# Masked sixteen-head attention: the mask is added on VectorE and on GpSimd instead of by matmuls

## The chip, the cores and the metric

The kernel runs on one core of one Trainium2 chip, as one launch. The metric is the device time of the program in microseconds. Five engines work beside each other, each through its own instructions in order: TensorE (PE in the profile; its weight loads are PEld), VectorE (DVE), ScalarE (ACT), GpSimd (POOL) and SyncE (SP), which issues the DMAs here. They wait for each other by semaphores. PE writes only to PSUM, eight banks of 128 x 512 float32; POOL works in SBUF.

## The reference

The program is a stack of twelve layers on a stream of 8 sequences of 256 tokens with 128 features. The change touches one of them, the second attention layer, which has 16 heads of 8 features and a causal mask:

```python
def _L1_attn_ref(x, w_qkv, b_qkv, w_out, b_out):
    N_HEADS = 16
    D_HEAD = D_MODEL // N_HEADS
    ...
    scores = jnp.einsum('bhqd,bhkd->bhqk', q, k) * scale
    causal = jnp.tril(jnp.ones((T, T), dtype=bool))
    scores = jnp.where(causal, scores, jnp.finfo(scores.dtype).min)
    attn = jax.nn.softmax(scores, axis=-1)
    out = jnp.einsum('bhqk,bhkd->bhqd', attn, v)
```

Two later layers have an attention of the same shape without a mask, over two members, and share the code.

## The kernel before

A class `SmallHeads` (L922) holds the attention of both kinds. `L1Attend` (L1268) is the masked one: `causal` is true, and there are 8 units, one for each sequence. The unmasked ones have 16 units each. All engines walk through one list of steps (`steps`, L974): step s belongs to unit s // 16 and head s % 16, and each engine emits its share of a step in the same order. So the order of the work is written out by hand, and an engine that waits holds up all its later work.

In the masked stage the 256 queries of a head are two blocks of 128, and the upper right block of the scores is never computed. A head has therefore three blocks of 128 columns: queries 0 with keys 0, queries 1 with keys 0, and queries 1 with keys 1. The first and the third need a triangular mask. The work of one unit goes like this:

- **Scores** (L1052 to L1064), one head in each step. PE writes the three blocks to bank 0 or 1, in turn. First a matmul of a bf16 identity (L1060) puts the mask table `mask_q` (0 or -3e38, 384 columns) into PSUM; two matmuls of 128 and 256 columns then add the scores. Before it writes, PE waits until the head two steps back has had its maximum taken (`topped`).
- **Maxima** (L1150): one DVE instruction for each head takes the maximum of each of the three blocks, from PSUM. After the last head, L1154 joins the second and third. POOL then splits the maxima into three bf16 parts (L1180 to L1186), PE turns them at step 3 of the next unit (L1023), and two DMAs add them as rows to the stacked keys and queries.
- **Shifted scores** (L1065 to L1080): at every odd step, 25 steps behind, PE computes the transposed scores less the maximum for a pair of heads, in banks 2 and 3 or 4 and 5, again with two mask matmuls first (L1075, table `mask_k`). ACT takes the exponential of both heads in one instruction (L1134) into one of four buffers `pt`.
- **Weighted values** (L1081 to L1097): once for two pairs, a quad, three steps behind its second pair, PE multiplies the exponentials with the values, sixteen matmuls.
- In between lie, on PE, the projections of a later unit (step 0), transposes (steps 5 and 9), the values (step 7) and the output (step 11); on DVE, the division at step 5 (L1159, L1162) and the addition to the stream at step 11 (L1306).
- POOL also splits queries and keys of a later unit into bf16 parts at step 0 (L1194 to L1201), behind the maxima.

SP carries the DMAs through DRAM that stack these parts. Stages are separated by a barrier of all engines.

## Time and profile before

| What | Value |
|---|---|
| Time, median of 3 runs | 2663.89 us |
| Lowest and highest run | 2650.3 and 2668.25 us |
| Time of the profiled execution | 2663.19 us |
| Span of the profiled execution, first to last instruction | 2661.4 us |
| Mean granted TensorE clock over the span | 0.877 |
| Busy: PE, PEld | 2029.5, 1075.7 us |
| Busy: DVE, ACT, POOL | 1438.6, 1142.0, 542.3 us |
| Masked stage, first maximum to last addition to the stream | 1351.5 to 1522.7 us |

The busy times are sums over the whole span, in which stages with very different loads follow each other. The granted clock is a share of 2.4 GHz; 0.5 is 1.2 GHz. Matmuls are pipelined, so a row's duration overlaps the next one's, and the time that a matmul takes from the engine is read from one start to the next. The profiled execution's own time exceeds its span by 1.8 us.

### The profile page before, as it was taken

How to read it: one execution, taken by the hardware profiler on the slowest of the kernel's cores; microseconds unless marked ns; L12 is line 12 of the kernel's file. 1: busy time of each engine (PE TensorE's matmuls, PEld its weight loads, DVE VectorE, ACT ScalarE, POOL GpSimd, SP SyncE). 2: the span in 40 equal slices, each digit the busy share in tenths (PEclk: the TensorE clock that was granted, in tenths of full speed). 3: DMA queues.
4: the chain of work that ended last, by engine and by line, in shares of the span. 5: the costliest groups of instructions: out<-in, count | busy, mean ns of one | idle time of the engine just before them, and what ended most of it. 6: DMA issues, size and time to landing. Idle time of an engine off the chain costs nothing.

```text
span 2661.4 us, 39085 instructions
## 1 busy us (share of the span) xinstructions
PE 2029.5 (76%) x15216; PEld 1075.7 (40%) x15216; DVE 1438.6 (54%) x2439; ACT 1142.0 (43%) x2404; POOL 542.3 (20%) x679
## 2 busy tenths in 40 slices
PE   6786877787877777868779965558798866689885
PEld 3444334433344523444334433224344443334444
DVE  4553465433555345533745367754677554477745
ACT  3454244421344424443424442223476623256761
POOL 2331134200233113320022000001332120223202
PEclk9998999888899799989879986788799977689997
DMA  3000000000000000000043000000544120154402
GB/s 134 1 1 1 0 1 1 1 0 0 1 1 1 1 0 1 1 1 1 0 91 61 2 0 0 0 0 8 106 83 88 23 64 0 33 97 79 91 7 80
DMA packets 50159, 70.97 MB, mean 27 GB/s; under 512 B 4980, under 2 KB 37972, under 8 KB 49464
## 3 DMA queue, kind: packets, MB, share of 16 engines
q1 hardware_dynamic: 47416, 60.07, 10.5%
q0 software_dynamic: 2560, 8.39, 1.0%
q8 instruction: 123, 2.02, 0.3%
q14 instruction: 60, 0.49, 0.1%
HBM read 50.59 MB, written 16.88 MB: 25 GB/s over the span
## 4 chain that ended last, share of the span: by engine, by line
PE 60%; DVE 20%; ACT 8%; issue 6%; POOL 4%; DMA 2%; SPq 0%; POOLq 0%; DVEq 0%; ACTq 0%
PE ps L196 57%; DVE arena L1150 3%; DVE arena L569 2%; PE ps L432 2%; ACT arena L516 1%; POOL arena L671 1%; POOL arena L664 1%; DVE arena L280 1%; ACT arena L269 1%; PE ps L1033 1%; DVE arena L642 1%; ACT arena L525 1%; DVE arena L915 1%; DVE arena L917 1%; ACT arena L270 1%
## 5 line engine op out<-in xcount | busy, mean ns | idle before, releaser
L196 PE MATMUL ps<-arena 128*18 128x256 f32 (+10 forms) x10088 | 716.1, 312 | 196.4 <-DVE arena L1150 47.7
L196 PEld LDWEIGHTS ps<-arena 128*18 128x18 f32 (+6 forms) x10088 | 388.0, 127 | 507.8 <-issue 180.3
L1150 DVE TENSOR_REDUCE arena<-ps 128x2 f32<-128x512 f32 (+1 forms) x640 | 396.3, 659 | 234.6 <-PE ps L196 232.0
L196 PE MATMUL ps<-arena,w_L0f 128*128 128x512 f32 (+3 forms) x800 | 356.1, 584 | 93.0 <-DVE arena L580 28.3
L1134 ACT ACTIVATE arena<-ps 128x1024 f32<-128x1024 f32 (+1 forms) x320 | 312.9, 981 | 132.9 <-PE ps L196 131.3
L516 ACT ACTIVATE arena<-ps,arena 128x128 f32<-128x128 f32 x512 | 227.0, 459 | 113.3 <-DVE arena L613 113.2
L196 PEld LDWEIGHTS ps<-arena,w_L0f 128*128 128x128 f32 (+2 forms) x800 | 153.1, 207 | 255.6 <-issue 160.2
L196 PE MATMUL ps<-arena,const 128*4 128x128 f32 (+2 forms) x1096 | 210.7, 416 | 35.9 <-ACT arena L1473 19.5
L671 POOL TENSOR_TENSOR arena<-arena 128x512 f32<-128x512 f32 x128 | 133.0, 1039 | 317.8 <-DVE arena L585 317.8
L569 DVE TENSOR_TENSOR arena<-ps,arena 128x1024 f32<-128x1024 f32 x128 | 152.6, 1219 | 64.1 <-PE ps L196 35.3
L525 ACT ACTIVATE arena<-ps 128x512 f32<-128x512 f32 x128 | 76.0, 598 | 225.3 <-PE ps L196 225.3
L663 POOL TENSOR_TENSOR arena<-arena 128x512 f32<-128x512 f32 x64 | 81.0, 1266 | 417.8 <-DVE arena L569 417.8
L196 PEld LDWEIGHTS ps<-arena,const 128*4 128x4 f32 (+2 forms) x1096 | 96.8, 108 | 141.3 <-issue 54.2
L280 DVE RECIPROCAL arena<-arena 4x128 f32<-4x128 f32 x80 | 67.7, 899 | 150.7 <-ACT arena L273 150.7
L432 PE MATMUL ps<-const,arena 128*128 128x128 f32 x512 | 91.5, 308 | 70.1 <-POOL arena L671 67.1
L580 DVE COPY arena<-ps 128x512 f32<-128x512 f32 x128 | 88.0, 688 | 96.1 <-PE ps L432 96.1
L196 PE MATMUL ps<-masks_b,ident_b 128*128 128x256 bf16 (+1 forms) x512 | 118.7, 315 | 25.9 <-ACT arena L516 15.1
L611 DVE TENSOR_REDUCE arena<-ps 128x8 f32<-128x1024 f32 x64 | 77.6, 1212 | 105.8 <-PE ps L196 105.4
L432 PEld LDWEIGHTS ps<-const,arena 128*128 128x128 f32 x512 | 64.9, 155 | 127.5 <-POOL arena L671 100.6
L516 ACT ACTIVATION_READ_ACCUMULATOR arena<-ps,arena 128x1 f32 x512 | 105.7, 206 | 0.0
L196 PE MATMUL ps<-arena,tilerow 4*128 4x128 f32 x672 | 88.2, 288 | 13.4 <-DVE arena L280 7.1
L196 PE MATMUL ps<-w_L0f,arena 128*128 128x512 f32 x192 | 97.6, 619 | 0.4
(231 smaller groups left out, 2403.5 us busy)
## 6 DMA issues: line engine op xcount, KB each, us to landing
scratch<-arena SPq DMA_DIRECT2D x40, 384.0 KB, 2.8
arena<-scratch SPq DMA_DIRECT2D x80, 192.0 KB
arena<-scratch SPq DMA_DIRECT2D x80, 128.0 KB
arena<-scratch SPq DMA_DIRECT2D x80, 88.0 KB
w_L0f<-in_L0f SPq DMA_DIRECT2D x2, 1557.0 KB, 12.4
arena<-arena SPq DMA_DIRECT2D x80, 12.0 KB
const<-in_const SPq DMA_DIRECT2D x1, 1276.0 KB, 7.9
residual<-in_x SPq DMA_DIRECT2D x1, 1024.0 KB, 5.0
```

What stands on the lines that cost most here:

```text
L196: return self.nc.tensor.matmul(o, lhsT, rhs, start=start, stop=stop, skip_group_check=True)
L280: V.reciprocal(r4, r4).then_inc(self.inverted.sem, 1)
L432: o = k.nc.tensor.transpose(k.ps[:, 6, (2 * j + t) * P:(2 * j + t + 1) * P], self.prob[G % 2][:, 2 * p + j, t, :], k.K("ident"))
L516: o = S.activation(self.prob[G % 2][:, j, t, :], k.ps[:, j, t * P:(t + 1) * P], ACT.Exp, bias=self.negm[G % 2][:, at:at + 1], scale=rn[:, ...
L525: self.k.nc.scalar.activation(self.sq[i % 4], self.k.ps[:, 4 + i % 2, :], ACT.Square).then_inc(self.squared.sem, 1)
L569: self.k.nc.vector.tensor_tensor(self.prod[n % 3].rearrange("p t (b s) -> p t b s", b=PER), x, tab, ALU.mult).then_inc(self.rotated.sem, 1)
L580: self.k.nc.vector.tensor_copy(self.probT[q % 4].rearrange("p j t s -> p (j t s)"), self.k.ps[:, 6, :]).then_inc(self.turn_copied.sem, 1)
L611: ch.did(V.tensor_reduce(self.mx[G % 2], ps[:, 0:4, 0:SEQ].rearrange("p j (t s) -> p j t s", t=2), AXX, ALU.max))
L663: G.tensor_tensor(y[:, i, :], first[:, 0, :], second[:, 1, :], ALU.add).then_inc(self.placed.sem, 1)
L671: self.k.nc.gpsimd.tensor_tensor(pr, pr, rinv, ALU.mult).then_inc(self.scaled.sem, 1)
L1134: S.activation(self.pt[g % 4][:, :, 0:both], ps[:, bank:bank + 2, 0:both], ACT.Exp, scale=self.scale).then_inc(self.exped.sem, 1)
L1150: V.tensor_reduce(self.mx[k % 2][:, :, at:at + 1], ps[:, i % 2, 0:SEQ + self.n1].rearrange("p (t s) -> p t s", t=self.blocks), AXX, ALU.ma ...
```

## The change

In the masked stage no matmul writes a mask any more.

For the maxima, DVE runs two instructions for each head in place of one. Each adds a part of the table `mask_q` (bf16, in SBUF) to the scores in PSUM, writes the sum as bf16 to a small buffer `masked`, and writes the maximum of the sums, with -3e38 as the start value, to one column: the first over 128 columns, the second over 256. That is one maximum for each block of queries, so L1154 and its flag `mx_joined` go.

For the exponentials, ACT exponentiates the unmasked shifted scores. POOL then overwrites, in place, the entries of the first and third block in which the key comes after the query with zeros, by one `affine_select` for each pair of 128 partitions x 512 float32. The weighted values wait for this (`selected`), and stand two steps further behind. POOL's loop runs over steps instead of units, and its splits stand at step 0, in the same order as before. The unmasked stages get the same instructions as before.

```diff
--- before.py
+++ after.py
@@ -925,6 +925,7 @@
 
 
 
+
     PAIRS, QUADS, LAG = HEADS // 2, HEADS // 4, 25
     STACKS, ROWS = STACKS, KD * len(SLOTS)
 
@@ -940,9 +941,9 @@
         self.qk = [a.take(2 * SEQ).rearrange("p (x s) -> p x s", x=2) for _ in range(2)]
         self.rest = a.take(2 * SEQ).rearrange("p (x s) -> p x s", x=2)
         self.parts = a.take_bf16(2 * PARTS * SEQ).rearrange("p (a s) -> p a s", a=2 * PARTS)
-        self.blocks = 3 if causal else 2
+        self.masked = a.take_bf16(2 * 3 * P).rearrange("p (e s) -> p e s", e=2)
         self.va = [a.take(2 * HEADS * 3 * (KD + 1)).rearrange("p (n d) -> p n d", n=2 * HEADS) for _ in range(3)]
-        self.mx = [a.take(self.blocks * HEADS).rearrange("p (t h) -> p t h", t=self.blocks) for _ in range(2)]
+        self.mx = [a.take(2 * HEADS).rearrange("p (t h) -> p t h", t=2) for _ in range(2)]
         self.mx_rest = a.take(2 * HEADS).rearrange("p (x g) -> p x g", x=4)
         self.mx_parts = [a.take_bf16(2 * PARTS * HEADS).rearrange("p (x a g) -> p x a g", x=4, a=PARTS) for _ in range(2)]
         self.mx_rows = [a.take_bf16(SEQ, PARTS * HEADS) for _ in range(2)]
@@ -958,9 +959,8 @@
         self.projected, self.biased, self.low = (self.sig(n, U) for n in ("projected", "biased", "low"))
         self.valued, self.v_copied = self.sig("valued", U), self.sig("v_copied", U)
         self.scored, self.topped = self.sig("scored", H * U), self.sig("topped", H * U)
-        self.mx_joined = self.sig("mx_joined", U)
         self.mx_split, self.mx_turned, self.mx_copied = (self.sig(n, U) for n in ("mx_split", "mx_turned", "mx_copied"))
-        self.shifted, self.exped = (self.sig(n, self.PAIRS * U) for n in ("shifted", "exped"))
+        self.shifted, self.exped, self.selected = (self.sig(n, self.PAIRS * U) for n in ("shifted", "exped", "selected"))
         self.weighed = self.sig("weighed", self.QUADS * U)
         self.raw_copied, self.turned, self.scaled, self.turned_again, self.ctx_copied = (
             self.sig(n, U) for n in ("raw_copied", "turned", "scaled", "turned_again", "ctx_copied"))
@@ -983,8 +983,9 @@
 
     def quad_at(self, s):
 
-        w = (s - self.LAG - 5) // 4
-        return w if s % 4 == 2 and 0 <= w < self.QUADS * self.units else None
+        s -= self.LAG + (7 if self.causal else 5)
+        w = s // 4
+        return w if s % 4 == 0 and 0 <= w < self.QUADS * self.units else None
 
     def is_unit(self, u):
         return 0 <= u < self.units
@@ -1056,11 +1057,9 @@
                     stacked = self.stacked[k % self.STACKS]
                     eng.wait_ge(stacked.sem, stacked.at(16 * self.loads * (k // self.STACKS + 1)))
                 self.wait_ge(eng, self.topped, s - 1)
-                if self.causal:
-                    mm(ps[:, e, 0:3 * P], k_.ident_b[:], k_.mask_q, stop=False)
                 for t in range(2):
                     keys = SEQ if t else self.n1
-                    o = mm(ps[:, e, t * self.n1:t * self.n1 + keys], q[rows, i // 2, t * P:(t + 1) * P], kk[rows, i // 2, 0:keys], start=not self.causal)
+                    o = mm(ps[:, e, t * self.n1:t * self.n1 + keys], q[rows, i // 2, t * P:(t + 1) * P], kk[rows, i // 2, 0:keys])
                 o.then_inc(self.scored.sem, 1)
             g = self.pair_at(s)
             if g is not None:
@@ -1070,18 +1069,15 @@
                     stacked = self.mx_stacked[u % self.STACKS]
                     eng.wait_ge(stacked.sem, stacked.at(32 * (u // self.STACKS + 1)))
                 self.wait_ge(eng, self.exped, g - 1)
-                if self.causal:
-                    for e in range(2):
-                        mm(ps[:, bank + e, 0:3 * P], k_.ident_b[:], k_.mask_k, stop=False)
                 for t, (st, cnt, at) in enumerate(((0, SEQ, 0), (SEQ - self.n1, self.n1, SEQ))):
                     for e in range(2):
                         rows = slice(64 * e, 64 * e + self.ROWS + PARTS)
-                        o = mm(ps[:, bank + e, at:at + cnt], kk[rows, x, t * P:(t + 1) * P], q[rows, x, st:st + cnt], start=not self.causal)
+                        o = mm(ps[:, bank + e, at:at + cnt], kk[rows, x, t * P:(t + 1) * P], q[rows, x, st:st + cnt])
                 o.then_inc(self.shifted.sem, 1)
             w = self.quad_at(s)
             if w is not None:
                 u, x = w // self.QUADS, w % self.QUADS
-                self.wait_ge(eng, self.exped, 2 * w + 2)
+                self.wait_ge(eng, self.selected if self.causal else self.exped, 2 * w + 2)
                 if w == 0:
                     self.wait_ge(eng, self.opened, 1)
                 if x == 0:
@@ -1147,11 +1143,13 @@
                 if i == 0:
                     self.wait_ge(eng, self.mx_split, k - 1)
                 at = self.PAIRS * (i % 2) + i // 2
-                V.tensor_reduce(self.mx[k % 2][:, :, at:at + 1], ps[:, i % 2, 0:SEQ + self.n1].rearrange("p (t s) -> p t s", t=self.blocks), AXX, ALU.max).then_inc(self.topped.sem, 1)
-                if self.causal and i == HEADS - 1:
-                    self.wait_ge(eng, self.topped, s + 1)
-                    mx = self.mx[k % 2]
-                    V.tensor_tensor(mx[:, 1, :], mx[:, 1, :], mx[:, 2, :], ALU.max).then_inc(self.mx_joined.sem, 1)
+                mx = self.mx[k % 2][:, :, at:at + 1]
+                if self.causal:
+                    for t, (st, end) in enumerate(((0, P), (P, 3 * P))):
+                        o = V.tensor_tensor_reduce(self.masked[:, i % 2, st:end], ps[:, i % 2, st:end], self.k.mask_q[:, st:end], 1.0, MASKED, ALU.add, ALU.max, mx[:, t])
+                else:
+                    o = V.tensor_reduce(mx, ps[:, i % 2, :].rearrange("p (t s) -> p t s", t=2), AXX, ALU.max)
+                o.then_inc(self.topped.sem, 1)
             u = k - 3
             if i == 5 and self.is_unit(u):
                 self.wait_ge(eng, self.turned, u + 1)
@@ -1167,16 +1165,18 @@
 
     def heads_gpsimd(self, eng, ch):
         G, U = self.k.nc.gpsimd, self.units
-        for k in range(-2, U + 1):
+        for s, k, i in self.steps():
+            g = self.pair_at(s)
+            if self.causal and g is not None:
+                pt = self.pt[g % 4][:, :, 0:3 * P].rearrange("p h (b c) -> p h b c", b=3)[:, :, 0:3:2]
+                self.wait_ge(eng, self.exped, g + 1)
+                G.affine_select(pt, pt, [[0, 2], [0, 2], [1, P]], ALU.is_ge, 0.0, base=0, channel_multiplier=-1).then_inc(self.selected.sem, 1)
             u = k - 1
-            if self.is_unit(u):
+            if i == 0 and self.is_unit(u):
                 mx, parts = self.mx[u % 2], self.mx_parts[u % 2]
-                if self.causal:
-                    self.wait_ge(eng, self.mx_joined, u + 1)
-                else:
-                    self.wait_ge(eng, self.topped, HEADS * (u + 1))
+                self.wait_ge(eng, self.topped, HEADS * (u + 1))
                 self.wait_ge(eng, self.mx_turned, u - 1)
-                mx = mx[:, 0:2].rearrange("p t (e g) -> p (t e) g", e=2)
+                mx = mx.rearrange("p t (e g) -> p (t e) g", e=2)
                 ch.did(G.tensor_copy(parts[:, :, 0, :], mx))
                 ch.wait_ge()
                 ch.did(G.tensor_tensor(self.mx_rest, mx, parts[:, :, 0, :], ALU.subtract))
@@ -1185,7 +1185,7 @@
                 ch.wait_ge()
                 G.tensor_tensor(parts[:, :, 2, :], self.mx_rest, parts[:, :, 1, :], ALU.subtract).then_inc(self.mx_split.sem, 1)
             u = k + 2
-            if self.is_unit(u):
+            if i == 0 and self.is_unit(u):
                 qk = self.qk[u % 2]
                 self.wait_ge(eng, self.biased, u + 1)
                 if u:
```

## Rows read from the trace of the kernel before

**Rows 1.** Busy us by stretch: PE, PEld, DVE, ACT, POOL; then the granted clock
```profile
1340.00:1360.00 20.00, 9.46 (x35) 3.18 (x34) 4.99 (x9) 1.24 (x3) 7.04 (x8) 0.50 0.65 140
...
1400.00:1420.00 20.00, 20.00 (x179) 8.59 (x177) 9.93 (x20) 9.17 (x14) 4.43 (x8) 1.00 0.30 64
1500.00:1520.00 20.00, 17.75 (x208) 7.87 (x206) 3.00 (x9) 12.30 (x18) 0.91 (x4) 1.00 0.01 3
```

**Rows 2.** The chain of waits in the masked stage: start us, length us
```profile
1412.24 14.57 PE ps L196 x128
```

**Rows 3.** Timeline of PE: start us, length us; two heads and a pair
```profile
1436.66 0.34 PE L196 MATMUL ps<-masks_b,ident_b 128*128 128x384 bf16 x1
1436.93 0.34 PE L196 MATMUL ps<-arena 48*128 48x128 bf16 x2
...
1437.73 0.50 PE L196 MATMUL ps<-masks_b,ident_b 128*128 128x384 bf16 x2
1438.17 0.34 PE L196 MATMUL ps<-arena 51*128 51x256 bf16 x4
1438.44 0.34 PE L196 MATMUL ps<-masks_b,ident_b 128*128 128x384 bf16 x1
```

**Rows 4.** Timeline of POOL: first instruction of the split of maxima, four units
```profile
1366.38 0.21 POOL L1180 CAST arena<-arena 128x32 bf16<-128x32 f32 x1 [11.30 <-DVE arena L1154]
...
1420.94 0.21 POOL L1180 CAST arena<-arena 128x32 bf16<-128x32 f32 x1 [14.70 <-DVE arena L1154]
...
1441.22 0.21 POOL L1180 CAST arena<-arena 128x32 bf16<-128x32 f32 x1 [14.70 <-DVE arena L1154]
...
1500.18 0.21 POOL L1180 CAST arena<-arena 128x32 bf16<-128x32 f32 x1 [18.20 <-DVE arena L1154]
```

**Rows 5.** Timeline of DVE: the first maximum of the masked stage
```profile
1351.51 0.56 DVE L1150 TENSOR_REDUCE arena<-ps 128x3 f32<-128x384 f32 x1 [19.04 <-PE ps L196]
```

**Rows 6.** Groups by form, masked stage: busy us, mean ns, idle before
```profile
L1150 DVE TENSOR_REDUCE arena<-ps 128x3 f32<-128x384 f32 x128 | 71.1, 559 | 89.5 <-PE ps L196 89.4
...
L1197 POOL TENSOR_TENSOR arena<-arena 128x512 f32<-128x512 f32 x8 | 9.2, 1155 | 0.6
...
L1194 POOL CAST arena<-arena 128x512 bf16<-128x512 f32 x8 | 4.9, 609 | 26.3 <-ACT arena L1109 17.4 <-DMA scratch<-arena 8.9
...
L1306 DVE SCALAR_TENSOR_TENSOR residual<-ps,cols,residual 128x256 f32<-128x256 f32 x8 | 3.8, 478 | 9.1 <-PE ps L196 9.1
...
L1162 DVE TENSOR_TENSOR arena<-ps,arena 128x256 f32<-128x256 f32 x8 | 3.4, 424 | 0.3
...
L1159 DVE RECIPROCAL arena<-ps 128x32 f32<-128x32 f32 x8 | 2.8, 351 | 9.6 <-PE ps L1033 9.6
```

**Rows 7.** Groups by form, whole kernel: operations near the new ones
```profile
L516 ACT ACTIVATION_READ_ACCUMULATOR arena<-ps,arena 128x1 f32 x512 | 105.7, 206 | 0.0
...
L285 DVE TENSOR_TENSOR arena<-arena,ps 128x512 f32<-128x512 f32 x64 | 41.4, 662 | 3.3 <-PE ps L196 3.1
...
L762 DVE SCALAR_TENSOR_TENSOR arena<-ps,cols,arena 128x512 f32<-128x512 f32 x32 | 24.0, 750 | 41.2 <-ACT arena L749 41.2
...
L627 DVE TENSOR_TENSOR stream<-stream,ps 128x256 f32<-128x256 f32 x32 | 13.4, 418 | 67.4 <-PE ps L196 67.4
...
L842 DVE TENSOR_TENSOR_SCAN arena<-arena 128x512 f32<-128x512 f32 x4 | 4.9, 1223 | 5.6 <-POOL arena L854 5.6
```

**Rows 8.** Timeline of POOL: split of maxima in the unmasked stage, two units apart
```profile
1927.16 0.21 POOL L1180 CAST arena<-arena 128x32 bf16<-128x32 f32 x1 [9.09 <-DVE arena L1150]
...
1957.16 0.21 POOL L1180 CAST arena<-arena 128x32 bf16<-128x32 f32 x1 [9.10 <-DVE arena L1150]
```

**Rows 9.** Busy us by stretch, unmasked stage, columns as in the first group
```profile
1920.00:1940.00 20.00, 17.98 (x196) 8.80 (x192) 14.55 (x25) 14.87 (x20) 4.44 (x8) 1.00 0.50 96
```

**Rows 10.** Busy us by stretch, earlier stages, columns as in the first group
```profile
380.00:400.00 20.00, 13.07 (x134) 8.21 (x134) 13.45 (x22) 9.86 (x34) 5.27 (x5) 1.00 0.00 1
860.00:880.00 20.00, 13.33 (x180) 9.90 (x180) 8.31 (x17) 6.50 (x28) 4.16 (x4) 0.83 0.00 1
```

## The prediction

> **What bounds the kernel now.** I read the time by stretch first. Only the masked attention layer changes, about 171 us of a 2661.4 us span. In its steady part PE is busy for all of 20.00 us, at a granted clock of 1.00, while DVE works 9.93, ACT 9.17 and POOL 4.43 us [rows 1]. The chain of waits agrees: it stays on PE for 14.57 us and 128 matmuls without a break [rows 2]. DVE waits for PE: 128 maxima of 559 ns are 71.1 us of work and 89.5 us of idle time in front [rows 6]. So the masked stage is bound by PE, and the question is what binds it when the mask matmuls are gone, and how soon.
>
> Its clock of units is the start of POOL's split of the maxima, which follows the last maximum of a unit: a unit takes 1441.22 - 1420.94 = 20.3 us, and the seven units after the first take 1500.18 - 1366.38 = 133.8 us [rows 4]. The first takes 1366.38 - 1351.51 = 14.9 us [rows 5]; it has only scores and maxima, at half the clock [rows 1]. After that comes a tail to 1522.7 us, 22.5 us, with shifted scores and weighted values alone.
>
> **What PE sheds.** From start to start, a head's mask takes 1436.93 - 1436.66 = 0.27 us, and a pair's two take 1438.17 - 1437.73 = 0.44 us [rows 3]. A unit has 16 heads and 8 pairs: 16 x 0.27 + 8 x 0.44 = 7.8 us. All of it lies on the path now. PE keeps 20.3 - 7.8 = 12.5 us of work in a unit. Nothing is added to PE.
>
> **What DVE takes on.** In place of 0.559 us for a head come two instructions, over 128 and over 256 columns, each with PSUM and SBUF as inputs. Two kinds of rows are near. A TENSOR_TENSOR with such inputs takes 0.418 us for 256 columns and 0.662 for 512, so 0.95 ns for a column and about 0.30 us for 128; the two together 0.72 us. A SCALAR_TENSOR_TENSOR takes 0.478 us for 256 and 0.750 for 512, 1.06 ns for a column, about 0.34 us for 128; together 0.82 us [rows 6, 7]. The first is the lower bound, and for the body I take the middle, 0.77. Keeping a running maximum should not slow it: today's maximum reads 384 columns in 0.559 us.
>
> Each of the two also has to write its maximum out. No DVE row shows that. On ACT the same thing is a row of its own, 0.206 us for one column [rows 7]. The bounds are 0 (it is part of the body, as in today's maximum) and 0.21 us for each; I take 0.1, since DVE's fixed cost is the smaller one: its body of 128 columns is 0.30 us in all. That makes 0.77 + 2 x 0.1 = 0.97 us for a head, with ends at 0.72 and 0.82 + 0.42 = 1.24.
>
> The Trainium skill says in "VectorE: DVE Perf Modes", section "Two Vector instructions with no wait between them", that an operation that also writes its accumulator is two instructions, the main one and an accumulator read. It gives no time for the read, and no trace here shows one on DVE; it speaks for the upper half of the range, and by it with ACT's price a head would cost about 1.2 us and the change would gain nothing.
>
> **The new unit.** DVE's other work in it is 0.35 + 0.42 + 0.48 = 1.25 us (L1159, L1162, L1306 [rows 6]). So DVE needs 16 x 0.97 + 1.3 = 16.8 us, more than PE's 12.5. PE is one head ahead of DVE (two banks), so it has about 2 x 0.97 us for a score of 0.27 and whatever stands beside it, and most insertions fit. The stage becomes bound by DVE. The join L1154 goes; it is worth 0.2 us, behind the last maximum, and nothing waits long for it.
>
> **POOL and the new wait.** A select reads one input of 512 elements. The nearest rows are POOL's one-input CAST of that size, 0.609 us, and its TENSOR_TENSOR, 1.155 us [rows 6]; below 0.6 nothing speaks for it, above 1.2 only an unknown. I take 0.85. Eight of them and today's 4.4 us [rows 1] are 11.2 us in a unit of 16.8. The wait falls on PE, in front of a quad, and behind it on PE stand all later scores. A quad stands five steps after its second pair, about 5 us, of which pair, ACT's exponential (0.8 us) and select use 2.2. It is tight once in a unit: at step 0 POOL does both splits, about 5 us, before it gets to the selects of steps 1 and 3, whose quad stands at step 8. POOL is then done at about 2.5 + 1.1 + 3.8 + 2 x 0.85 = 9.1 us after the last score of the unit before, and step 8 comes at 9 x 1.05 = 9.4. So I cost the wait at nothing; its cover is DVE's slowness, and if DVE is fast it may cost up to 0.5 us a unit. The later split of the maxima is not late either: it waits for the select of step 15 first, at most 0.85 us, and PE wants it only at step 3. SP's queue and its DMAs are untouched.
>
> The Trainium skill, "GPSIMD Engine Reference", section "4.1 Engine selection", calls one-input operations on GpSimd roughly line-rate and two-input ones about twice as slow; CAST and TENSOR_TENSOR here stand at 0.61 and 1.16 us, which agrees, and by it a select would be near 0.6. The sum would not move, as DVE sets the pace.
>
> **The sum.** First unit: 16 x 0.97 = 15.5 for 14.9 us, +0.6. The second and third have no division and no addition yet, 15.5 each, and the second stalls on projections at half the clock, for which I add 1.5: 32.5. The other five take 16.8: 84.0. Together 116.5 for 133.8, -17.3. The tail has 12 pairs; their masks are 12 x 0.44 = 5.3 us, but its PE is busy only 17.75 of 20 us and ACT 12.30 [rows 1], and the last select adds 0.85. Between -5.3 and +1 I take -2. Sum: 0.6 - 17.3 - 2 = -18.7 us. From the profiled execution's own 2663.19 us that gives 2644.5; the median before, 2663.89, is 0.7 above it, so I say **2645 us**. The change of slope is the thing to know: 0.1 us on a head of DVE is 128 x 0.1 = 12.8 us.
>
> **Rivals.**
>
> Fast DVE. The read-out is nearly free, a head costs 0.72 to 0.90 us. Then DVE's 16 x 0.8 + 1.3 = 14.1 us meets a floor. The unmasked stage shows it: two units take 30.0 us [rows 8], so 15.0 each, with PE at 17.98 and DVE at 14.55 of 20 us [rows 9], that is 13.5 and 10.9 in a unit. The hand-over costs 1.5 us beyond the busier engine. Here PE's 12.5 + 1.5 = 14.0 is the floor. Six units in 14.1 to 14.5 instead of the 118.5 they take now, and 2 to 3 us in the rest: -34 us, **2629**. For it speaks that all today's maxima are free of a second row.
>
> Dear DVE, slower than before. From 0.97 + 18.7/128 = 1.12 us a head the gain is gone, and from 1.32 the kernel is slower by over 1%. If the new instruction runs at the rate of TENSOR_TENSOR_SCAN, 1.223 us for 512 columns [rows 7] against 0.69 for other forms, 384 columns cost 0.4 us more: 1.37 us a head, -18.7 + 128 x 0.40 = +32, **2696**. Against it speaks the 0.559 us of today's maximum. This also covers that the "one instruction" is executed as several.
>
> Slow select. From (16.8 - 4.4 - 1.2) / 8 = 1.4 us a select POOL sets the pace (1.2 for its waits), through the wait in front of the quads. At 2.0 us a unit takes 21 to 22, about +8 us; at 2.4 it is 25 and **2695**. Against it speak both POOL rows; for it, only that no select is in the trace.
>
> Cold PE. With PE busy for 12.5 of 16.8 us the granted clock could stay at 1.2 GHz, as in the first unit. PE would need 23 to 25 us a unit: **2700**. In earlier stages 13.07 busy of 20 us go with a clock of 1.00, and 13.33 with 0.83 [rows 10], so dips are possible, but PE's own slack of 4 us covers these.
>
> **Chances.** Forecast (0.90 to 1.12 us a head, 2639 to 2664): 0.48. Fast DVE: 0.27. Dear DVE: 0.15, of which 0.06 beyond 1%. Slow select 0.06, half of it beyond 1%. Cold PE 0.04. A change under 1% (26.6 us) can hardly be told from none here, the runs before spread over 18 us. Faster by over 1%: the fast DVE and the lower edge of the forecast, 0.32. Slower by over 1%: 0.06 + 0.03 + 0.04 = 0.13. Within: 0.55. The range goes from the fast rival, 2629, less 2 for scatter, to 1.24 us a head, 2679: 2627 to 2680.
>
> **What would show it.** The two new rows on DVE and their sum for a head (0.97), any row for the read-out; DVE busy at over 18 of 20 us in the steady part and PE near 15; a unit of 16.8 us by POOL's splits; selects near 0.85 us, and no wait of PE for POOL above some tenths; the tail 2 us shorter. The prediction is wrong if a head on DVE is off by 0.1 us or more, if PE waits for POOL in every unit, or if the clock falls in the steady part.

## The result and the profile after

| | Before | After |
|---|---|---|
| Median beside each other, 4 runs each | 2661.99 us | 2619.82 us |
| Ratio to before, 95% interval | | 0.9834 [0.9802, 0.9865] |
| Profiled execution, span | 2661.4 us | 2615.4 us |
| Mean granted clock | 0.877 | 0.874 |
| First maximum to last addition | 171.2 us | 129.8 us |

The change makes the kernel 1.7% faster. The ratios are the recorded ones with their intervals; the quotient of the two medians, 0.984 here, lies inside the interval each time. One execution of e1_dve_part took 6265.98 us where its other three took 2620 to 2639, and it is left out below. 2645 was forecast; the time lies 7 us below the lower end of the range, and on the side of the fast-DVE rival (2629).

I read the profile after in the order in which the argument went before. First the time by stretch (columns: window, its length, busy us of PE, PEld, DVE, ACT, POOL with instruction counts, granted clock, DMA share, GB/s):

```profile
1340.00:1360.00 20.00, 10.68 (x46) 4.17 (x46) 10.57 (x71) 1.24 (x3) 5.98 (x10) 0.50 0.68 131
1360.00:1380.00 20.00, 18.32 (x142) 9.08 (x140) 13.76 (x91) 9.76 (x15) 11.88 (x19) 0.53 0.46 98
...
1400.00:1420.00 20.00, 16.13 (x216) 9.02 (x204) 14.84 (x95) 11.90 (x20) 15.16 (x26) 1.00 0.41 81
1420.00:1440.00 20.00, 16.49 (x214) 8.67 (x208) 15.55 (x99) 12.57 (x19) 8.09 (x16) 0.91 0.25 53
```

In the steady part nobody is busy all the time: PE has fallen from 20.00 of 20 us [rows 1] to 16.1, and DVE stands at 14.8, not at the 18 that a DVE-bound stage would show. The clock comes later than before: read in stretches of 2 us, it reaches 1.00 about 18 us after the first maximum in the kernel before and about 34 us after it here. The chain of waits (start us, length us) says the same. One unbroken piece of PE [rows 2] has become an alternation:

```profile
1398.98 1.54 PE ps L196 x22
1400.52 0.02 issue
1400.55 1.21 DVE arena L1149 x8
1401.76 0.05 issue
1401.81 1.11 PE ps L196 x18
...
1405.33 1.90 PE ps L196 x26
```

The clock of units, the start of POOL's split of the maxima, against [rows 4]:

```profile
1357.41 0.21 POOL L1180 CAST arena<-arena 128x32 bf16<-128x32 f32 x1 [6.94 <-DVE arena L1149]
...
1399.64 0.21 POOL L1180 CAST arena<-arena 128x32 bf16<-128x32 f32 x1
...
1413.37 0.21 POOL L1180 CAST arena<-arena 128x32 bf16<-128x32 f32 x1
...
1454.75 0.21 POOL L1180 CAST arena<-arena 128x32 bf16<-128x32 f32 x1
```

A steady unit takes 1413.37 - 1399.64 = 13.7 us for 20.3; seven units take 97.3 for 133.8, which is -36.5. The first, from the first maximum at 1346.46, takes 10.95 for 14.9: -3.9. The tail takes 21.5 for 22.5: -1.0. Together -41.4. The span of the profiled execution is 46 us shorter. The other 4.6 are 5.0 gained ahead of the first maximum and 0.4 lost behind the stage, where but for a fraction of a microsecond nothing is changed: in the experiments below, except e14, all with the same code ahead of the stage, the first maximum comes anywhere from 1340.9 to 1351.0 us. The two medians lie 42.2 us apart, about what the stage gave.

Now the rows that answer to the costs, groups by form in the masked stage (busy us, mean ns):

```profile
L1149 DVE CUSTOM_DVE_ANT_0 arena<-ps,masks_b 128x256 bf16<-128x256 f32 x128 | 53.7, 419 | 0.0
...
L1173 POOL TENSOR_SCALAR_AFFINE_SELECT arena<-arena 128x512 f32<-128x512 f32 x64 | 40.4, 637 | 43.8 <-ACT arena L1130 43.5
L1149 DVE CUSTOM_DVE_ANT_0 arena<-ps,masks_b 128x128 bf16<-128x128 f32 x128 | 36.9, 288 | 43.9 <-PE ps L196 43.0
...
L1149 DVE DVE_READ_ACCUMULATOR2_ANT arena<- 128x1 f32 x256 | 21.2, 83 | 0.0
```

By durations a head costs 288 + 83 + 419 + 83 = 873 ns, within a tenth of the 0.97 us that I forecast. But the timeline of DVE (start us, length us) shows how these rows lie:

```profile
1397.15 0.42 DVE L1149 CUSTOM_DVE_ANT_0 arena<-ps,masks_b 128x256 bf16<-128x256 f32 x1
1397.49 0.09 DVE L1149 DVE_READ_ACCUMULATOR2_ANT arena<- 128x1 f32 x1
1397.49 0.29 DVE L1149 CUSTOM_DVE_ANT_0 arena<-ps,masks_b 128x128 bf16<-128x128 f32 x1
1397.70 0.08 DVE L1149 DVE_READ_ACCUMULATOR2_ANT arena<- 128x1 f32 x1
1397.70 0.42 DVE L1149 CUSTOM_DVE_ANT_0 arena<-ps,masks_b 128x256 bf16<-128x256 f32 x1
1398.05 0.08 DVE L1149 DVE_READ_ACCUMULATOR2_ANT arena<- 128x1 f32 x1
```

The next instruction begins before the row in front of it has ended, and the read-out begins at the same moment as the next instruction. From start to start the 128 columns take 0.21 us and the 256 columns 0.35: **0.555 us for a head**. That is what the single maximum took, 0.559 [rows 6]. DVE needs 16 x 0.555 + 1.25 = 10.1 us in a unit, less than PE's 12.5. PE itself is busy for 11.6 of the 13.7 us, so even 12.5 was high by this measure.

So neither engine sets the 13.7 us alone. The waits between 1380 and 1460 us (engine, line, waited for: us in total, times, longest) show what is left of PE's idle time:

```profile
POOL arena L1173 <- ACT arena L1130: 33.1, 36, 2.1
...
PE ps L196 <- DVE arena L1160: 6.9, 5, 1.4
...
PEld ps L196 <- POOL arena L1186: 5.5, 6, 1.9
...
PE ps L196 <- POOL arena L1186: 3.7, 3, 1.6
...
PEld ps L196 <- POOL arena L1173: 0.9, 6, 0.2
```

Once a unit PE stands 1.4 us at step 7, for the division of DVE. The split of the maxima, wanted at step 3, makes PE wait 1.0 to 1.6 us only at the start of the last two units and of the tail; in the steady units only weight loads wait for it, 0.37 us. PE does not wait for the selects (0.9 us for weight loads, in six pieces). POOL waits for ACT, so the selects are early enough.

### The profile page after: what moved, and what is told of

Same layout as the page of the kernel before. It is cut to its first block, busy times and chain, and to the rows that moved or that the text cites. A ratio compares the mean times of both kernels' runs of the same rounds, so it can differ in the third digit from the quotient of the medians.

```text
span 2615.4 us, 39014 instructions
## 1 busy us (share of the span) xinstructions
PE 1962.8 (75%) x14960; PEld 1058.9 (40%) x14960; DVE 1442.4 (55%) x2815; ACT 1140.4 (44%) x2404; POOL 582.3 (22%) x743
## 4 chain that ended last, share of the span: by engine, by line
PE 58%; DVE 21%; ACT 8%; issue 7%; POOL 4%; DMA 2%; SPq 0%; POOLq 0%; DVEq 0%; ACTq 0%
PE ps L196 54%; DVE arena L1151 3%; DVE arena L569 2%; PE ps L432 2%; ACT arena L516 2%; POOL arena L671 1%; POOL arena L664 1%; DVE arena L280 1%; ACT arena L269 1%; PE ps L1034 1%; DVE arena L642 1%; ACT arena L525 1%; DVE arena L915 1%; DVE arena L1149 1%; DVE arena L917 1%
## 5 line engine op out<-in xcount | busy, mean ns | idle before, releaser
L196 PE MATMUL ps<-arena 128*18 128x256 f32 (+10 forms) x10088 | 699.1, 314 | 216.8 <-DVE arena L1151 47.6
L1151 DVE TENSOR_REDUCE arena<-ps 128x2 f32<-128x512 f32 x512 | 325.6, 686 | 145.5 <-PE ps L196 143.0
L1149 DVE CUSTOM_DVE_ANT_0 arena<-ps,masks_b 128x128 bf16<-128x128 f32 (+1 forms) x256 | 76.3, 354 | 43.9 <-PE ps L196 43.0
```

The lines of the kernel that those rows point to most:

```text
L196: return self.nc.tensor.matmul(o, lhsT, rhs, start=start, stop=stop, skip_group_check=True)
L1149: o = V.tensor_tensor_reduce(self.masked[:, i % 2, st:end], ps[:, i % 2, st:end], self.k.mask_q[:, st:end], 1.0, MASKED, ALU.add, ALU.max, ...
L1151: o = V.tensor_reduce(mx, ps[:, i % 2, :].rearrange("p (t s) -> p t s", t=2), AXX, ALU.max)
```

## The experiments

Theory A: DVE's real price of a head is 0.555 us, start to start, so DVE does not bind, and PE's missing 7.8 us of mask matmuls become time up to the waits for POOL's split and the division. Rival B (my forecast): DVE costs 0.9 us and more and sets the pace; the gain then came from elsewhere, a warmer clock or a shorter unit for another reason. Rival C: the select or its later quad decides.

All figures beside the ratios are from the profiled execution of each, in us: the first unit from first maximum to split, the seven units after it (the second to the eighth in the text), the stage from first maximum to last addition.

| Kernel | Median | Ratio to before, 95% | First unit | Seven units | Stage |
|---|---|---|---|---|---|
| before | 2661.99 | 1 | 14.9 | 133.8 | 171.2 |
| after | 2619.82 | 0.9834 [0.9802, 0.9865] | 10.95 | 97.3 | 129.8 |
| e1_dve_part | 2631.86 | 0.9856 [0.9782, 0.993] | 10.96 | 108.6 | 142.5 |
| e2_pool_part | 2653.2 | 0.9954 [0.9925, 0.9983] | 14.87 | 123.5 | 159.8 |
| e3_one_by_one | 2653.46 | 0.9966 [0.9939, 0.9992] | 14.7 | 130.3 | 167.4 |
| e4_third_instruction | 2666.81 | 1.0006 [0.9976, 1.0037] | 15.02 | 135.7 | 173.0 |
| e5_select_twice | 2637.57 | 0.9919 [0.9891, 0.9947] | 10.94 | 115.5 | 151.5 |
| e6_quad_lag5 | 2644.38 | 0.9936 [0.9909, 0.9962] | 10.95 | 117.0 | 156.9 |
| e7_quad_halves | 2627.19 | 0.9874 [0.9812, 0.9937] | 10.95 | 103.8 | 137.3 |
| e8_no_select | 2615.53 | 0.9831 [0.9776, 0.9885] | 10.94 | 97.2 | 127.3 |
| e9_split_first | 2631.33 | 0.9819 [0.98, 0.9839] | 10.94 | 99.4 | 130.0 |
| e10_split_first_turn4 | 2623.52 | 0.9796 [0.978, 0.9813] | 10.95 | 95.5 | 126.4 |
| e11_third_and_filler | 2680.18 | 1.0019 [0.9996, 1.0042] | 17.05 | 135.6 | 174.2 |
| e12_third_small_filler | 2677.81 | 1.0058 [1.0029, 1.0088] | 15.02 | 151.7 | 188.0 |
| e13_changed_again | 2625.75 | 0.9857 [0.9814, 0.99] | 10.95 | 100.0 | 132.3 |
| e14_split_turn_warm | 2618.23 | 0.984 [0.9803, 0.9876] | 14.68 | 89.6 | 123.7 |
| e15_split_turn_again | 2611.14 | 0.982 [0.9785, 0.9856] | 10.95 | 96.8 | 127.2 |

The kernel before took 2657.7 to 2675.43 us beside these, by the chip; medians of different groups (e1 to e4, e5 to e8, e9 to e11, e12 to e15) are compared by their ratios only.

**The two halves of the change.** Changed kernel, mask matmuls of the pairs back, no select:

```diff
+                if self.causal:
+                    for e in range(2):
+                        mm(ps[:, bank + e, 0:3 * P], k_.ident_b[:], k_.mask_k, stop=False)
...
-            if self.causal and g is not None:
+            if False and g is not None:
```

> Only the maxima are changed: the new DVE instructions and no mask_q matmuls; the mask_k matmuls stay, POOL selects nothing, quads three steps behind as before. Theory (a head costs DVE 0.56 us from start to start, so PE stays the bound and each PE saving counts fully): PE sheds 16 x 0.27 = 4.3 us of a 20.3 us unit, units of 16.0 to 16.2 us, first unit about 4 us shorter as in the changed kernel, about -33 us against the kernel before, 2629. Rival (a head costs DVE 0.87 us, the sum of its four rows): units of 16 x 0.87 + 1.3 = 15.2 us would still hide under PE, first unit 14 us instead of 11, so about -30. The two lie close here; the run is for what the maxima alone are worth beside the whole change. A second rival: POOL's part is what gave the time, and this run stands within 10 us of the kernel before.

The other half: the old maximum with its mask matmul and join, but the select of POOL:

```diff
+                    mm(ps[:, e, 0:3 * P], k_.ident_b[:], k_.mask_q, stop=False)
...
+                V.tensor_reduce(self.mx[k % 2][:, :, at:at + 1], ps[:, i % 2, 0:SEQ + self.n1].rearrange("p (t s) -> p t s", t=self.blocks), AXX, ALU.max).then_inc(self.topped.sem, 1)
```

> Only the exponentials are changed: no mask_k matmuls, POOL selects, quads five steps behind; the maxima are as before, with mask_q matmuls and the join. Theory: PE sheds 8 x 0.44 = 3.5 us of a 20.3 us unit, but the hand-over between PE and DVE shows again as PE has less to do; units of 16.8 to 17.7 us, first unit unchanged at 14.9, about -18 to -23 us against the kernel before, 2640 to 2645. Rival (POOL's select and its wait cost PE time): units stay above 18.5 us and the gain under 12 us.

Time by stretch, first of e1, then of e2:

```profile
1400.00:1420.00 20.00, 19.97 (x210) 9.37 (x204) 13.59 (x86) 11.52 (x18) 5.28 (x12) 1.00 0.44 81
```

```profile
1400.00:1420.00 20.00, 19.24 (x195) 9.69 (x194) 11.52 (x24) 10.99 (x18) 11.60 (x24) 1.00 0.31 65
```

With DVE's two instructions alone the unit is 15.75 us and PE is full; DVE at 0.97 us a head would have made it 16.8. Here DVE has 5 us of slack in a unit. With the select alone the unit is 16.82, which is 20.3 less eight pairs of 0.44. Both are in the main bound by PE (it is idle for 0.8 of the 16.82 us), and both sizes of what PE sheds were about right: 20.3 - 4.3 = 16.0 forecast for e1, 15.75 measured. The stage saves 28.7 and 11.4 us, together 40.1 of the change's 41.4, but this sum is partly luck. In a steady unit the halves save 4.5 + 3.5 = 8.0 us and the whole change only 6.6, as its waits come in; and e2 loses 6.6 us in its second and third units, which grow from 15.26 and 19.01 us to 19.03 and 21.80. There PE is busy all the time at a clock of 0.50 and 0.66, where the kernel before had 0.90 and 1.00. Without them e2's stage would be 18 us shorter, the lower end of what was expected. Why the clock came later there is open. The first unit's 3.9 us come with the DVE part alone.

**DVE at the price that I forecast.** In e3 each of DVE's instructions waits for the one before:

```diff
                 if self.causal:
+                    self.wait_ge(eng, self.topped, s)
                     for t, (st, end) in enumerate(((0, P), (P, 3 * P))):
                         o = V.tensor_tensor_reduce(...)
+                        if t == 0:
+                            ch.did(o)
+                            ch.wait_ge()
```

> The changed kernel with a wait in front of each of the two DVE maxima, so that each starts only when the one before it, its read-out included, has completed. Theory (what the forecast missed is that the rows overlap: a head is 0.288 + 0.083 + 0.419 + 0.083 = 0.87 us by durations but 0.555 us from start to start): with the overlap forbidden a head costs 0.87 us plus two semaphore delays of about 0.05, 0.97 us, which is the forecast's own figure; units of 16 x 0.97 + 1.3 = 16.8 us, first unit 15.5, about +25 us against the changed kernel, 2645. Rival (the forecast failed elsewhere, for instance because DVE is not what bounds the stage at such a cost): under +10 us.

```profile
1416.03 0.29 DVE L1150 CUSTOM_DVE_ANT_0 arena<-ps,masks_b 128x128 bf16<-128x128 f32 x1
1416.25 0.08 DVE L1150 DVE_READ_ACCUMULATOR2_ANT arena<- 128x1 f32 x1
1416.36 0.42 DVE L1150 CUSTOM_DVE_ANT_0 arena<-ps,masks_b 128x256 bf16<-128x256 f32 x1
1416.71 0.08 DVE L1150 DVE_READ_ACCUMULATOR2_ANT arena<- 128x1 f32 x1
1416.94 0.29 DVE L1150 CUSTOM_DVE_ANT_0 arena<-ps,masks_b 128x128 bf16<-128x128 f32 x1
```

The rows are as long as in the changed kernel, 0.29, 0.08, 0.42 and 0.08, yet the head now takes 1416.94 - 1416.03 = 0.91 us instead of 0.555. So the durations say nothing of the pitch; the overlap does. Two units of this kernel, by stretch:

```profile
1413.10:1429.30 16.20, 12.33 (x144) 6.84 (x136) 12.63 (x67) 8.52 (x14) 9.26 (x17) 0.92 0.39 79
1429.30:1450.20 20.90, 17.31 (x162) 8.33 (x160) 12.70 (x68) 8.95 (x14) 9.45 (x18) 0.65 0.30 61
```

The first is what I forecast, 16.2 us for 16.8, with PE's 12.3 of 12.5 in it. In the second DVE works the same 12.7 us, but the granted clock is at 0.65, PE's work stretches from 12.3 to 17.3 us, and the unit takes 4.7 more. The clock fell with PE idle for 3.9 of 16.2 us. My "cold PE" rival, given 0.04, is a real mechanism once DVE sets the pace. It is not confined to that case: the changed kernel's seventh unit stands at 0.88, and at 0.79 in e13.

**A third instruction**, the 256 columns once more, into a buffer that nobody reads, without a wait:

```diff
+                        if t:
+                            V.tensor_tensor_reduce(self.again[:, i % 2, :], ps[:, i % 2, st:end], self.k.mask_q[:, st:end], 1.0, MASKED, ALU.add, ALU.max, self.mx_again[:, i % 2:i % 2 + 1])
```

> The changed kernel with a third DVE maximum for each head, over 256 columns, into a buffer that nothing reads, between the two. Theory (price from start to start, 0.345 us for the 256-column one): a head costs 0.90 us, DVE 16 x 0.90 + 1.3 = 15.7 us of a unit and becomes the bound, units of 15.7 to 16.3, about +16 to +19 us against the changed kernel, 2636 to 2639. Rival (price by durations, 0.50 us more on 0.87): 1.37 us a head, units of 23 us, over +60 us.

```profile
1412.57 0.42 DVE L1151 CUSTOM_DVE_ANT_0 arena<-ps,masks_b 128x256 bf16<-128x256 f32 x1
1412.91 0.08 DVE L1151 DVE_READ_ACCUMULATOR2_ANT arena<- 128x1 f32 x1
1412.91 0.42 DVE L1152 CUSTOM_DVE_ANT_0 arena<-ps,masks_b 128x256 bf16<-128x256 f32 x1
```

```profile
1420.00:1440.00 20.00, 16.10 (x146) 8.14 (x146) 15.45 (x98) 8.90 (x14) 8.94 (x16) 0.67 0.32 64
```

The third costs its 0.35 us, as theory A says. What was expected of the time (2636 to 2639) failed: the clock is at 0.67 in the steady part and all of the change's gain is gone, though DVE is busy for only 15.5 of 20 us.

**Can the clock be held by filler?** e11 adds to e4 a matmul of 384 columns ahead of each head's scores, e12 one of 128 columns from the second unit on:

```diff
+                if self.causal:
+                    mm(ps[:, e, 0:3 * P], k_.ident_b[:], k_.mask_q)
...
+                if self.causal and k:
+                    mm(ps[:, e, 0:P], k_.ident_b[:], k_.mask_q[:, 0:P])
```

> The kernel with a third DVE instruction for each head (units of 19 to 20.5 us at a granted clock of 0.67, 2667 us), with one more matmul of 384 columns on PE in front of each head's scores, whose result the scores overwrite. It is work added: 16 x 0.27 = 4.3 us a unit for PE at full clock. Theory (in that kernel the excess over DVE's 15.7 us a unit comes from PE at 1.2 GHz, which falls there because PE is idle too often): PE stays at 2.4 GHz, its 12.5 + 4.3 = 16.8 us is the bound, units of 16.8 to 17.5 us, and the kernel gets faster by 10 us or more through added work, to 2645 to 2655. Rival (the excess is DVE's instruction or the hand-over, not the clock): slower than without the filler, 2667 or more.

> The kernel with a third DVE instruction for each head (units of 19 to 20.5 us, granted clock 0.67), with a small filler on PE: a matmul of 128 columns in front of each head's scores from the second unit on, about 0.12 us at full clock, 1.9 us a unit; the scores overwrite its result. The filler of 384 columns brought the clock back to 1.00 for part of the stage and units from 20.5 to 18.3 us, but cost PE 4.3 us a unit itself. Theory (the excess over DVE's 15.7 us is PE at 1.2 GHz, and a little more work on PE holds it at 2.4 GHz): units of 15.8 to 16.8 us wherever the clock reads 1.00, 15 us or more off the kernel without filler, about 2645 to 2650. Rival: the clock stays at 0.67, units of 20 us or more, 2667 or more.

```profile
1420.00:1440.00 20.00, 18.08 (x135) 9.11 (x136) 15.04 (x92) 8.10 (x12) 6.70 (x11) 0.65 0.33 64
```

No: in e12 PE is busy for 18.1 us and the clock stays at 0.65. From the fourth on, the units grow from e4's 19.2 to 20.5 to 22.6 to 23.7 us, though DVE has no more to do. So at that clock PE is in the main the bound (busy for 21.3 of 23.3 us), which is why slack on PE is no cover. With 384 columns the clock is at 1.00 in the middle (units of 18.3 us), but the filler costs as much as it brings, and e11 ends where e4 did.

**The select and its quad.** e5 runs the select twice, e8 never, e6 sets the quad back to its old distance, e7 computes it in two halves, two steps apart:

```diff
+                ch.did(G.affine_select(pt, pt, [[0, 2], [0, 2], [1, P]], ALU.is_ge, 0.0, base=0, channel_multiplier=-1))
+                ch.wait_ge()
...
-        s -= self.LAG + (7 if self.causal else 5)
+        s -= self.LAG + 5
...
-                    for f in range(4):
+                    for f in (range(2 * half, 2 * half + 2) if self.causal else range(4)):
```

> The changed kernel with every select run twice, the second behind the first. Each takes 0.64 us, so a pair costs POOL about 1.3 us and a unit 8 x 1.3 + 4.9 = 15.6 us. Theory A (POOL has slack now, with 8 x 0.64 + 4.9 = 10.0 of 13.7 us, but none for twice the work): POOL's wait in front of the quads becomes the bound, units of 15 to 16 us, about +12 to +15 us against the changed kernel, 2632 to 2635. Theory B (the quads' wait is far from the path, as the forecast costed it at nothing): under +3 us.

> The changed kernel with quads three steps behind their second pair, as before the change, instead of five. Theory: the exponential (0.8 us) and the select (0.64 us) do not fit in three steps of 0.86 us, and after POOL's splits at step 0 the selects are late, so PE waits for POOL in every quad or at least once in a unit; units of 15 to 16.3 us, +9 to +15 us against the changed kernel. Rival: PE's queue has slack of 2.5 us in a unit that takes this up, under +3 us.

> The changed kernel with the sixteen matmuls of a quad in two halves of eight, one for each pair, five steps behind the pair and two steps apart. Theory (the unit of 13.7 us is PE's 12.5 us of work plus a hand-over between PE and DVE, which shows because a whole quad, 0.78 us, stands between two scores while only two banks hold scores; half of it, 0.4 us, would fit beside a maximum of 0.555 us): units of about 13.2, -4 us against the changed kernel. Rival (earlier first halves run into POOL's splits, and the wait takes the place of the hand-over): units of 14 us or more, +3 us or more.

> The changed kernel without the selects: the quads wait for the exponentials alone, five steps behind, and the exponentials of masked places enter the weighted sums. This leaves POOL's new work and wait out. Theory (they are off the path while each select takes 0.64 us, but the split of the maxima stands behind the select of step 15): 0 to -4 us against the changed kernel, mostly in the tail and in the last two units. Rival (PE waits for POOL in every unit): units of 13.0 us or less, -6 us or more.

Without the select the steady units at a clock of 1.00 take the same 13.73 to 13.74 us: it costs nothing there. That the seven units sum to 97.2 us for 97.3 is chance. The second and the last two are 3.0 us shorter (of these the seventh stands at 0.88 in the changed kernel), and the sixth stands at a clock of 0.79 and takes 16.23 for 13.74. The tail is 2.4 us shorter, the stage 2.5. What the select costs at these edges is mostly the split behind it, since e9 below, with the select but the split ahead of it, gains nearly as much there. The ratio (0.9831) can't be told from the change's. Twice, the select makes POOL the busiest engine, and the clock falls too (0.83, later 0.55), so that e5's units, from the fourth on 15.5 to 19.1 us where 15 to 16 were expected, are not POOL's doing alone. e5 by stretch, then two waits of e6 from 1380 to 1460 us:

```profile
1380.00:1400.00 20.00, 16.42 (x205) 8.96 (x194) 13.41 (x87) 12.15 (x20) 18.53 (x32) 0.91 0.49 84
```

```profile
PEld ps L196 <- POOL arena L1173: 9.4, 14, 2.5
...
PE ps L196 <- POOL arena L1173: 4.2, 3, 2.3
```

With the quad at its old place PE waits for the select up to 2.5 us, and 0.010 of the ratio is lost. The long waits (1.7 and 2.3 us of PE) come right behind POOL's splits at step 0, for just the reason that the forecast gave. The waits alone don't make units of up to 20 us: in the third to the sixth, of 16.9 to 20.0 us, the clock stands at 0.50 to 0.82, and the last two, at 1.00 and 0.98, take 13.65 us. The two steps more are needed. The halves (e7) are slower than whole quads, with units of 15.34 us at a clock of 1.00, for a reason that nobody had expected. Groups by form, changed kernel and e7, the same 512 matmuls:

```profile
L196 PE MATMUL ps<-arena 128*18 128x256 f32 x256 | 21.8, 415 | 0.7 <-POOL arena L1173 0.7
...
L196 PE MATMUL ps<-arena 128*18 128x128 f32 x256 | 13.9, 291 | 0.0
```

```profile
L196 PE MATMUL ps<-arena 128*18 128x256 f32 x256 | 39.7, 389 | 5.2 <-POOL arena L1175 5.1
L196 PE MATMUL ps<-arena 128*18 128x128 f32 x256 | 25.1, 275 | 0.0
```

Busy time goes from 35.7 to 64.8 us: 32 whole quads take about 1.1 us each, 64 halves 1.0. These means mix both clocks. At a clock of 1.00 a whole quad (here of the kernel before) and a half (e7) look so in the timeline of PE:

```profile
1500.91 0.84 PE L196 MATMUL ps<-arena 128*18 128x256 f32 x16 [0.20 <-ACT arena L1134]
```

```profile
1406.96 0.83 PE L196 MATMUL ps<-arena 128*18 128x256 f32 x8 [1.20 <-POOL arena L1175]
```

Half the matmuls take as long as all. The four heads of a quad go to four groups of 32 columns, a half's two heads to two; that the four run beside each other would explain it, and no run separates it from other causes. The rival came true as well: PE waits 1.2 us for a select once a unit, in place of the 1.4 for the division. But PE's busy time grows by 2.3 us a unit, and the unit by 1.6.

**What holds 13.7 us.** e9 puts POOL's split of the maxima at step 15, ahead of that step's select; e10 also moves the transposes and the division from step 5 to step 4; e15 is e10 again, e13 the changed kernel again, on one chip:

```diff
-            u = k - 1
-            if i == 0 and self.is_unit(u):
+            u = k if self.causal else k - 1
+            if i == (15 if self.causal else 0) and self.is_unit(u):
...
-            if i == 5 and self.is_unit(u):
+            if i == (4 if self.causal else 5) and self.is_unit(u):
```

> The changed kernel with POOL's split of the maxima ahead of the select of step 15 instead of behind it. In the changed kernel's steady stretch (from 1380 to 1460 us) PE and PEld wait 3.7 and 5.5 us for the last split instruction L1186, at step 3. Theory (a part of the 13.7 us unit is this wait, because the split starts only when the last select is done, about 1 us after the last maximum): the wait goes, units of about 12.9 to 13.2 us where it stood, -3 to -7 us against the changed kernel. Rival (PE then waits as long at step 7, for the division that it waits for already, as it arrives there earlier): within 2 us of the changed kernel.

> As the run before, and PE's transposes and DVE's division one step earlier, at step 4, so that the division has three steps until PE writes the values to the same bank at step 7; PE waits 1.4 us there in each unit of the changed kernel. Theory (these two waits are all that stands between PE's 12.5 us of work and the unit of 13.7): both go, units of 12.3 to 12.7 us, -6 to -10 us against the changed kernel, near 2611. Rival (two banks of scores hold PE and DVE together, and what one wait gives back the next takes): -3 us or less.

> The changed kernel itself, on the same chip as the next two, so that they can be compared with it and not only with the kernel before. All theories: 0.982 to 0.985 of the kernel before.

> The kernel with the split first and the transposes at step 4 again, on the same chip as the changed kernel. Theory: both waits of PE were on the path, 5 to 8 us off the changed kernel, a ratio to it of 0.997 to 0.998. Rival: no difference beyond the scatter of the runs.

Waits of e9, then of e10, over the same stretch:

```profile
PE ps L196 <- DVE arena L1160: 6.8, 5, 1.4
...
PEld ps L196 <- POOL arena L1181: 1.7, 3, 1.0
```

```profile
PE ps L196 <- DVE arena L1160: 1.4, 4, 0.3
```

With the split first, the weight loads' wait for it falls from 5.5 to 1.7 us and the last units take 12.9 for 13.2 to 14.5, but steady ones still 13.73. With the division a step earlier its wait falls from 6.8 to 1.4 us and steady units take 12.97, the last 12.1. So the wait for the division holds the steady unit, and half of the 1.5 us of "hand-over" that I had carried over from the unmasked stage is that one wait. Part of this is lost early in the stage: in e9, e10 and e15 the third and fourth units take 16.1 to 17.8 us, at clocks of 0.61 to 0.74, where the changed kernel takes 14.7 or 15.9 and then 13.7. In time this version is probably a little ahead: beside the changed kernel 2611.14 to 2625.75 us. The intervals of the two ratios overlap (0.9785 to 0.9856 and 0.9814 to 0.99), but taken directly the six runs of each differ in the mean by 12.7 us, by my estimate with a 95% interval from 2 to 23. The profiles show 5.1 us of it in the stage (127.2 for 132.3), and 3.4 in the earlier pair (126.4 for 129.8). It is the fastest version found.

e14 is e10 with 30 matmuls of 512 columns ahead of the first scores and the 384-column filler in the first 25 steps, for a warm clock in the first units (0.50 and 0.53 in the changed kernel):

```diff
+                if self.causal and s == 0:
+                    for _ in range(30):
+                        mm(ps[:, 0, :], k_.ident_b[:], k_.masks_b[:, 0:BANK])
...
+                if self.causal and s < self.LAG:
+                    mm(ps[:, e, 0:3 * P], k_.ident_b[:], k_.mask_q)
```

> The kernel with the split first and the transposes at step 4, and PE kept busy where it has little to do: 30 matmuls of 512 columns while it waits for the first stacked keys (10.4 us idle now), and one of 384 columns in front of each of the first 25 heads' scores; the scores overwrite the results. Theory (the first four units run long, 12.8 to 16.4 us where later ones take 12.1 to 13.0, because PE is granted 1.2 GHz until about 1390 us): first unit 9.0 to 9.5 us instead of 10.95, units 2 to 4 at 12 to 13 us, 6 to 10 us off, about 0.976 of the kernel before. Rival (the clock falls again once the pairs begin, or the filler delays the first scores): within 3 us of the kernel without filler.

The seven units take 89.6 us for e15's 96.8, the first 14.7 for 10.95, and the first maximum comes 0.6 us later; the stage is 3.5 us shorter and the median 7 us longer than e15's. No gain is shown. Why the first unit grew, the clock tells, first ahead of the first maximum (at 1354.5), then behind it:

```profile
1346.00:1354.00 8.00, 4.58 (x22) 1.88 (x20) 0.00 (x0) 0.00 (x0) 2.91 (x3) 1.00 0.82 153
1356.00:1370.00 14.00, 14.00 (x48) 5.20 (x48) 9.02 (x56) 0.40 (x1) 2.87 (x6) 0.50 0.75 134
```

The 30 matmuls did bring the clock to 1.00, but it was back at 0.50 about a microsecond after the first maximum, with PE busy all the time from there, and the filler then cost PE as much as the old masks did. The rival in the expectation, that the clock falls again, is what came, and earlier than it said. What the seven units gain (7.3 us) is a clock that comes back about 18 us after the first maximum instead of 36.

## Why the prediction was wrong, step by step

**The step that failed** is "That makes 0.77 + 2 x 0.1 = 0.97 us for a head". Its terms were not far off as durations: 0.707 for the two bodies for 0.77, 0.083 for a read-out for 0.1. The error was to add them. Durations of rows are not what an engine needs for them: DVE's rows overlap, and from start to start a head takes 0.555 us, below the lower end of 0.72, which was made of durations too. Of the 0.415 us between 0.97 and 0.555, 0.2 are the read-outs, about 0.15 the overlap of the two bodies and 0.06 their sizes. The trace of before had what was needed. Its DVE rows overlap: a maximum at 1407.58 us has a row of 0.56 us, and the next instruction starts 0.48 us after it. And so do the ACT rows from which the 0.206 us for a read-out came, here at 421 us (start us, length us):

```profile
421.38 0.45 ACT L516 ACTIVATE arena<-ps,arena 128x128 f32<-128x128 f32 x1
421.72 0.20 ACT L516 ACTIVATION_READ_ACCUMULATOR arena<-ps,arena 128x1 f32 x1
421.81 0.45 ACT L516 ACTIVATE arena<-ps,arena 128x128 f32<-128x128 f32 x1
```

By durations the pair is 0.65 us, from start to start 421.81 - 421.38 = 0.43, less than its body alone. The prediction had read PE so, "from start to start". For DVE and for this read-out it did not ask.

From it followed "The stage becomes bound by DVE" and the unit of 16.8 us; 13.7 was measured. At that unit's size the step itself held: e3, with 0.91 us a head, has a unit of 16.2 us while the clock stands at 0.92. But even then the sum would have been wrong, in the other direction: "PE's own slack of 4 us covers these" fell in e3 and e4, where the clock went to 0.65 and 0.67 and the kernels took 2653 and 2667 us, not 2645.

**First unit**, "+0.6": -3.9 was measured. At the lower clock a head's mask takes as long as its scores, 0.43 us each, and the unit before had PE busy throughout. With DVE at 0.62 us a head, its waits for PE included, the unit sheds 16 x 0.25 = 3.9 us. e1 has all of it, e2 none.

**The fast-DVE rival** (0.27) named the right mechanism, a read-out that is nearly free, though its 0.72 to 0.90 us a head was too high as well. Its floor came out right, "PE's 12.5 + 1.5 = 14.0" for 13.7 measured, but in part by luck: PE is busy for 11.6 us of it and the rest is the wait for the division and smaller ones. Its 2629 is 9 us too high. The stage gave 41.4 us for its 34: its six units 35.0 for about 32.7, the rest 6.4 (3.9 of it the first unit) for 2 to 3. The other 2 us are the kernel before, whose median was 2661.99 in this comparison and 2663.89 in the forecast.

**What held.** PE sheds about 7.8 us in a unit (units 4.5 us shorter in e1 for 4.3, 3.5 in e2 for 3.5; by PE's busy time it is 8.7, 20.3 less 11.6). The maximum and the add in one pass run at the rate of plain forms, not of the scan: the dear-DVE rival is out. The tail, -1.0 for -2. The select is cheap, 0.637 us for the 0.85 taken, and hidden (e8), if its quad stands two steps later (e6); that POOL sets the pace from 1.4 us a select fits e5, where two in a row take 1.3 and POOL is busy for 18.5 of 20 us, but the lower clock stands beside it there. The wait for the late split of the maxima, "at most 0.85 us, and PE wants it only at step 3", was costed at nothing and is there in the last units, 1.0 to 1.6 us: with DVE fast, step 3 comes too soon. e9 takes most of it away.

The Trainium skill, "VectorE: DVE Perf Modes", section "Two Vector instructions with no wait between them", is right that the accumulator read is a row of its own; the estimate by ACT's price (1.2 us a head) that I hung on it was wrong, by the measured 83 ns that lie beside the next instruction. The same page of the Trainium skill says in "The DRAIN you can't avoid" both that the next operation waits until the pipe is empty and that one which isn't held starts earlier. The timelines agree with the second: the same rows at 0.555 us a head without a wait and at 0.91 with one. The Trainium skill, "GPSIMD Engine Reference", section "4.1 Engine selection", calls one-input operations roughly line-rate, and 0.637 us beside CAST's 0.609 [rows 6] agrees. The prediction compared its factor of about two for two-input ones with CAST; it is meant against VectorE, whose 0.662 us for 512 columns [rows 7] the 1.155 us exceed 1.7 times.

**What stays open.** Why the clock falls when it does. Read at full clock or nearly so, PE is busy for 12.3 of 16.2 us in e3, where it falls, for 11.6 of 13.7 in the changed kernel, where it falls in some units and not in others, and for 13.8 of 15.3 in e7, where from the third unit on it stays at 1.00. Why it reaches 1.00 only about 34 us after the first maximum in the changed kernel and 50 in e2, for 18 before, is open too. What a warm first unit would be worth is not shown, as e14's did not stay warm.

## What to carry to other kernels

Price an instruction by the distance to the next start in a back-to-back stretch of its engine's timeline, never by the duration of its row; two short instructions can cost no more than the long one they replace. When work is taken from PE and another engine becomes the bound, read the granted clock before counting PE's slack as cover: in e3 and e4 it fell to 0.65 and 0.67 and took most or all of the gain. Compare units at the same clock: two equal sums (e8) can hide a gain and a loss. After the bound moves, list what PE waits for once in each unit, and move those producers a step earlier; that is where the next microseconds were.

## What the runs showed of the hardware

- DVE's add-and-maximum from PSUM and SBUF takes 0.21 us for 128 columns and 0.35 for 256 from start to start, with the read-out of the maximum (83 ns) beside the next instruction. Waits on each predecessor raise the pair from 0.555 to 0.91 us (e3).
- Eight matmuls to two groups of 32 columns take as long on PE (0.83 us, e7) as sixteen to four groups (0.84 us, the kernel before), both at a granted clock of 1.00.
- The granted clock was 0.65 to 0.67, between the levels of 1.2 and 2.4 GHz as a mean over 20 us, in stretches with PE busy for 16 to 18 of 20 us (e3, e4, e12), and 1.00 with 16.1 in the changed kernel. Busy time grows by itself at the lower level, so the share tells little of the load.
- In e14 the granted clock was 1.00 ahead of the first maximum and 0.50 about a microsecond behind it, and stayed there for 14 us in which PE was busy throughout.
- POOL's select in place over 128 x 512 float32 took 0.637 us.
